# Score rows placed later between the convolution's taps, and one normalised operand made by VectorE

## The reference, cut to what matters

```python
x = x + L0(_gn(x))                      # Mamba
x = x + L1(_gn(x))                      # relu(conv3x3(batchnorm(.))) + ., then conv1x1
x = x + L2(_gn(x))                      # attention, below
x = x + L3(_gn(x))                      # bilinear shift, then 1x1

def _gn(v, G=32, eps=1e-05):            # two channels of one image form a group
    ...
    return ((g - m) / jnp.sqrt(s + eps)).reshape(v.shape)

def _L2_conv_ref(x, w1, b1, a1, w2, b2, a2, wa, ba, aa):
    e1 = _conv1x1(x, w1, b1, a1).reshape(N, -1, HW)       # prelu(w1 x + b1), 32 channels
    e2 = _conv1x1(x, w2, b2, a2).reshape(N, -1, HW)
    asm = _conv1x1(x, wa, ba, aa).reshape(N, C, HW)
    score = jax.nn.softmax(jnp.einsum('nci,ncj->nij', e1, e2), axis=2)
    return jnp.einsum('nij,ncj->nci', score, asm).reshape(N, C, H, W)
```

## Time and profile before

| what | value |
|---|---|
| median of 3 runs | 696.53 us (693.73 to 700.42) |
| span of the profiled execution | 697.9 us |
| TensorE (PE) busy | 625.1 us, 90% |
| VectorE (DVE) busy | 535.1 us, 77% |
| ScalarE (ACT) busy | 429.5 us, 62% |
| GpSimd (POOL) busy | 385.2 us, 55% |
| chain that ended last, by engine | PE 58%, DVE 19%, issue 8%, ACT 7%, POOL 4% |
| mean granted TensorE clock | 0.972 of full speed |

### The profile page before, as it was taken

One profiled execution on the slowest core, in us unless ns is written; L12 is line 12 of the kernel. 1 busy time (PEld: TensorE's weight loads), 2 busy tenths in 40 slices (PEclk: granted clock), 3 DMA queues, 4 the chain that ended last, 5 costly groups with the idle time before them and its releaser, 6 DMA issues.

```text
span 697.9 us, 8622 instructions
## 1 busy us (share of the span) xinstructions
PE 625.1 (90%) x2812; PEld 275.6 (39%) x2812; DVE 535.1 (77%) x857; ACT 429.5 (62%) x737; POOL 385.2 (55%) x243
## 2 busy tenths in 40 slices
PE   3795888888789989999989999999999999986996
PEld 1232332233353332234434444343444444335982
DVE  6996899999934465888858787887878888685547
ACT  2478689899644331235555765748476565787772
POOL 2454788887512140216939779595968979430000
PEclk9997999999999997999989999999999999998999
DMA  9000000000015482404003040300304020200006
GB/s 328 7 0 0 1 0 0 0 0 0 1 45 140 112 199 54 106 1 91 0 1 90 1 91 0 71 21 9 83 0 91 0 31 1 30 1 0 1 1 241
DMA packets 28533, 32.36 MB, mean 46 GB/s; under 512 B 16976, under 2 KB 17104, under 8 KB 28368
## 3 DMA queue, kind: packets, MB, share of 16 engines
q1 hardware_dynamic: 27056, 27.33, 15.3%
q10 hardware_dynamic: 1440, 4.55, 2.7%
HBM read 5.83 MB, written 4.19 MB: 14 GB/s over the span
## 4 chain that ended last, share of the span: by engine, by line
PE 58%; DVE 19%; issue 8%; ACT 7%; POOL 4%; DMA 1%; SPq 1%; DVEq 0%; POOLq 0%; ACTq 0%
PE PS L1723 15%; PE PS L1710 10%; PE PS L1688 9%; PE PS L1599 5%; DVE RB L476 3%; PE PS L1608 2%; PE PS L1677 2%; PE PS L1743 2%; DVE RB L552 2%; DVE PS L544 2%; DVE RB L851 2%; DVE RB L559 1%; PE PS L1850 1%; DVE SM L456 1%; DVE SM L692 1%
## 5 line engine op out<-in xcount | busy, mean ns | idle before, releaser
L692 DVE TENSOR_REDUCE SM<-PS 128x1 f32<-128x512 f32 x256 | 165.0, 683 | 65.3 <-PE PS L1688 64.7
L1154 ACT ACTIVATE RB<-PS 128x512 f32<-128x512 f32 x256 | 138.9, 594 | 88.0 <-PE PS L1710 86.9
L1391 POOL TENSOR_TENSOR RB<-RB 128x1024 f32<-128x1024 f32 x60 | 141.1, 2372 | 7.1 <-DVE RB L721 4.8
L1710 PE MATMUL PS<-R 98*128 98x512 f32 x256 | 95.5, 452 | 1.3 <-ACT RB L1154 1.3
L1688 PE MATMUL PS<-R 96*128 96x512 f32 x256 | 88.7, 418 | 6.9 <-DMA R<-R 3.2
L1723 PE MATMUL PS<-RB 128*64 128x512 f32 x320 | 85.4, 616 | 0.0
L1710 PEld LDWEIGHTS PS<-R 98*128 98x128 f32 x256 | 38.8, 189 | 83.4 <-ACT RB L1154 53.9
L1526 PE MATMUL PS<-RA,W 128*128 (+1 forms) x128 | 63.1, 636 | 8.7 <-DVE RB L552 5.3
L1688 PEld LDWEIGHTS PS<-R 96*128 96x128 f32 x256 | 48.7, 193 | 43.1 <-DVE SM L692 18.9
L1391 POOL TENSOR_TENSOR EX<-EX,RB 128x1024 f32<-128x1024 f32 x24 | 56.5, 2373 | 0.8
L1723 PE MATMUL PS<-RB,RA 128*64 128x512 f32 x192 | 52.7, 627 | 0.0
(11 more groups left out here) (186 smaller groups left out, 1111.7 us busy)
## 6 DMA issues: line engine op xcount, KB each, us to landing
R<-WS SPq DMA_DIRECT2D x72, 128.0 KB, 2.4
X<-x SPq DMA_DIRECT2D x8, 512.0 KB, 7.4
RB<-RB SPq DMA_DIRECT2D x32, 128.0 KB, 4.0
RB<-RB ACTq DMA_DIRECT2D x14, 280.5 KB, 4.1
out<-X SPq DMA_DIRECT2D x7, 512.0 KB, 2.7
R<-R SPq DMA_DIRECT2D x20, 128.0 KB, 2.4
W<-pack SPq DMA_DIRECT2D x1, 1072.0 KB, 11.6
R<-R ACTq DMA_DIRECT2D x4, 128.0 KB, 3.3
```

The costliest lines, as they stand in the source:

```text
L692: v.tensor_reduce(MX[:, par, tile, h:h + 1], bank(2 + h), AX.X, ALU.max)\
L1154: act(slot[:, h * HALF:(h + 1) * HALF], bank(4 + h), ACT.Exp).then_inc(s["p_ready"], 1)
L1391: i = g.tensor_tensor(out, out, PT[j % SLOTS][par], ALU.add)
L1710: mm(bank(4 + h), stack(b, par, 1)[0:98, j * P:(j + 1) * P], stack(b, par, 0)[0:98, h * HALF:(h + 1) * HALF]).then_inc(s["t_mm"], 1)
```

## The change

Two edits.

`FILLS` becomes `{5: (7, 4), 6: (0, 14), 7: (0, 14)}`: the first rows of pair 0 stand at slot 7 of turn 5, not at slot 3, and turns 6 and 7 take 14 rows each, not 12 and 13. The 32 rows stay 32.

`GB[0]` of pair 3 is made by VectorE, right behind `coefs_shift(GN2B, ...)` and ahead of its part of `attend(1)`. It counts in a semaphore of its own, `gb_third`, for which TensorE waits ahead of `operands(3)`. The wait for `coef_ready`, which stood ahead of `normed(3)` on GpSimd, stands ahead of `normed(4)` and its followers.

```diff
--- before.py
+++ after.py
@@ -254,7 +254,7 @@
             return bank(7 if isinstance(p, int) and (p, h) == (PAIRS - 1, 1) else 5)
 
         SLOTS1 = 9
-        FILLS = {5: (3, 7), 6: (0, 12), 7: (0, 13)}
+        FILLS = {5: (7, 4), 6: (0, 14), 7: (0, 14)}
 
         def fills_at(p, slot):
 
@@ -298,7 +298,7 @@
             dt_mm b_mm c_mm o_mm v_mm e_done dta_read u_done dt_read nd_done ln_done dt_done dtx_done
             b_read da_done scan_done c_read hc_done y_done y_last sq_done r_done normed0 blk0_done sums_done
             g1_ready ua_done ub_first ub_done shifted_even shifted_odd moved_even moved_odd conv_mm y1_done w1_mm x1_done
-            minus_done gb_ready z_mm z_read zf_done hi_done lo_done stack_in stack_low asm_mm asm_done v_part v_done
+            minus_done gb_ready gb_third z_mm z_read zf_done hi_done lo_done stack_in stack_low asm_mm asm_done v_part v_done
             s_mm s_read m_ready
             mrow_mm m_copied t_mm p_ready pv_done first_added add_done add_dve sum_mm ln_sum rec_done acc_read x2_done
             g3_pool g3_dve g3_act hat_d hat_abs hat_done am_zero am_in am_dve am_act tr_mm tr_act tr_dve s1_mm s1_copied s2_mm s2_copied
@@ -825,6 +825,8 @@
                                                 6: lambda: end7(0), 7: lambda: link(end7(1)), 10: gather,
                                                 12: lambda: coefs_var(GN2B, 3, PAIRS)})
             coefs_shift(GN2B, 3, PAIRS)
+            v.wait_ge(s["asm_mm"], 2)
+            v.tensor_scalar(GB[0], X[:, 3, :], SC[:, 3:4], SH[:, 3:4], ALU.mult, ALU.add).then_inc(s["gb_third"], 1)
             for p in range(1, PAIRS - 1):
                 attend(p, p % 3)
 
@@ -1391,9 +1393,6 @@
                         i = g.tensor_tensor(out, out, PT[j % SLOTS][par], ALU.add)
                     i.then_inc(s["add_done"], 1)
                     g.wait_ge(s["add_done"], 6 * p + j - 1)
-                    if j == 7 and p == 0:
-                        g.wait_ge(s["coef_ready"], GN2B + 1)
-                        normed(3)
 
             def clear(k):
                 g.memset(RB[:, k * L:(k + 1) * L], 0.0).then_inc(s["am_zero"], 1)
@@ -1421,6 +1420,7 @@
             g.wait_ge(s["y1_done"], 2 * PAIRS)
             for p in range(PAIRS):
                 if 0 < p < PAIRS - 3:
+                    g.wait_ge(s["coef_ready"], GN2B + 1)
                     normed(p + 3)
                 if p == PAIRS - 2:
                     g.wait_ge(s["t_mm"], 32 * (PAIRS - 2))
@@ -1653,7 +1653,10 @@
 
             def operands_free(q):
 
-                t.wait_ge(s["gb_ready"], q + 1)
+                if isinstance(q, int) and q == 3:
+                    t.wait_ge(s["gb_third"], 1)
+                else:
+                    t.wait_ge(s["gb_ready"], q if q > 3 else q + 1)
                 if isinstance(q, int) and q < 2:
                     need(t, s["v_done"], 2 * q)
                 else:
```

## The result

The changed kernel takes 692.34 us in the median of 20 runs (689.05 to 694.53), the kernel before 698.85 us in the median of 20 (692.78 to 701.18). The ratio is 0.9915, with a 95% interval of 0.9897 to 0.9932: 5.9 us less by the ratio, 6.5 between the medians, and 7.8 us above the predicted 684.5, outside of the predicted range of 681 to 690.

What follows compares the result with a forecast made beforehand. TensorE was taken to lose time only at two waits and the half clock behind them. Gains of 7.8 and 5.0 us sum to 12.8, from 697.9 to 685.1; median put at 684.5 us, range 681 to 690.

Steps and rivals of the forecast that it cites:

- What bounds the kernel: TensorE stands still for nothing in the attention, 40.14 us from pair to pair; gains lie only at seam A and seam B.
- The rows later: Turn 5: row 0 moved to slot 7, reached after its operands land, so wait and clock fall go: -7.8 us.
- Rivals 2, 3 and 4: Turns 6/7 pauses drop clock, 689.1 (0.12); clock stays down, slower (0.04); stack late, wait moves to slot 7, 692 (0.04).
- seam A: Turn 5, first row of pair 0: TensorE idles 3.17 us for a stack DMA, then half clock; 7.8 us to win.
- I take the lower end, for two reasons: Operand on VectorE put at 0.81 us, not 3.2, because recorded starts put it ahead of GpSimd's addition.
- seam B: Step 2 of attend(1): TensorE waits for GpSimd's normed(3), then half clock; costs 5.4 us, forecast gain 5.0.
- The bound from above: The operand on VectorE waits out one whole GpSimd addition: 2.4 + 0.8 = 3.2 us.
- Rival 1: Seam B: GpSimd's addition goes first, TensorE idles 2.7 us; 686.8, or 689.7 if the clock falls; chance 0.2.
- the sum: Seam A and seam B together: -7.8 - 5.0 = -12.8 us, taking the profiled execution from 697.9 to 685.1.

Runs made afterwards that it cites:

- e2: Changed kernel with the old FILLS table, so only the operand of pair 3 moves to VectorE: 698.24 us, ratio 1.0009 to before.
- e1: Kernel before with only the new FILLS table, the operand of pair 3 staying on GpSimd: 691.03 us, ratio 0.9909 to before.
- e5: Changed kernel with a product of two SBUF tiles in place of the tensor_scalar, values of pair 3 wrong: 688.66 us, one run.
- e4: Kernel before with the new FILLS table and the operand still on GpSimd, one addition earlier: 687.16 us, ratio 0.9846 to before.
- e3: Changed kernel, but GpSimd holds its last two additions of pair 0 until VectorE has made the operand: 686.86 us, ratio 0.9850 to before.
- e10: e4 with a table that starts the rows at slot 5 of turn 5: 687.00 us, ratio 0.9830 to before.
- e7: Changed kernel, but ScalarE makes the operand of pair 3, behind the exponentials of step 0 of attend(1): 687.42 us, ratio 0.9863 to before.
- e8: Changed kernel, but VectorE makes the operand one step later, behind the maxima of step 0 of attend(1): 686.58 us, ratio 0.9855 to before.
- e9: e4 with a table that starts the rows at slot 6 of turn 5: 687.10 us, ratio 0.9833 to before.

## Why the prediction was wrong, point by point

**What bounds the kernel: right.** The `operands` of pairs 4 and 5 stay 40.10 to 40.15 us apart in all twelve profiles. What was won or lost stands at the two seams.

**"The rows later": right in mechanism and place.** No idle ahead of the first row; 1.11 and 0.41 us of pauses for 1.5 and 0.4; S1 is 8.2 us shorter for 7.8. Rivals 2, 3 and 4 did not come: in the profiled execution the clock stays at its upper level, 2.4 GHz, from 250 to 300 us, and the wait did not move to slot 7.

**The size of that term was high for a median run.** 4.6 of the 7.8 us was clock, read from one execution. e2 waits at the same place, for 3.22 us, and its clock costs far less: its S1 is 47.32, 3.0 less than before's 50.27 with the same distribution of the rows. So of 4.6 us it lost 1.6. e1's ratio puts the whole of seam A at 6.3 us (4.7 to 8.0). The prediction saw that a median run may have less to win, and took 0.8 us off for it: 684.5 is 12.0 below 696.53.

**The base was off by about two us.** The prediction set the span of 697.9 beside the median of 696.53 as 1.4 above. The span leaves out 1.8 us of the device's time, so this execution is 699.7, 3.2 above that median. Over 20 runs the median of before is 698.85, and the execution is 0.9 above it. Of three runs spread over 6.7 us the median is itself no better known than by some us.

**"I take the lower end, for two reasons" is the step that failed.** The term is the operand on VectorE, put at 0.81 us; it took 2.93, the maxima behind it came late, and seam B, put at -5.0 us, came to +1.7 in the profile. The bound from above was right: the tensor_scalar waits for a whole addition, 2.93 us against the bound of 3.2. Both reasons were read from recorded starts. "The new operation is 0.03 us behind it, ahead of the addition" came true to 0.01 us, and it lost nevertheless. The other, L429 at 29.78, was an operation on two slices of `SM` and without a scalar column, beside another operation of GpSimd. It is of the kind that won in e5; the new one is of the kind that lost in after and e2. Even without e5 the text could have seen that a margin of 0.03 us between two engines' records carries no decision, and it gave the other outcome 0.2.

**Rival 1's cost came, at its upper end,** though by the records the addition was not first. It had the operation at 3.2 us and the idle at 2.7; they are 2.93 and 1.99. With the clock's fall it had 689.7, that is 6.8 us below the 696.53 from which it started; measured are 6.5 below 698.85. So of the 2.6 us between 689.7 and 692.34 the base makes 2.3. Its single terms were off in both directions: the clock's part was put at 2.9 us, as in before, and in the profile of after S2 is 7.0 us over e4's floor of 84.95, of which 2.0 is the idle and 5.0 the clock (10 us at its lower level). That profile is the slowest run of after, so the median run lost less; that its single terms add up to the right total is in part luck.

**The seam's price was about right.** Where it does close (e3, e4), S2 falls by 4.8 and 5.35 us against before's 90.30, for the 5.0 of the sum. Both seams together, S1 and S2 of e4, are 13.5 us below before's, for 12.8. By its ratio e4 is 10.7 us faster (9.3 to 12.1): that is what the change could have brought. From e1 to e4, seam B alone, it is 3.9 in medians, for the 5.0 of the sum.

## What to carry to other kernels

An operation that moves from GpSimd to VectorE can stay on the same lock, as it did here: ask what GpSimd runs at that time, take the length of that instruction as the price, and do not decide by which of two records begins first. Look at what queues behind the moved operation before where it is needed; `GB[0]` had three us to spare, the maxima behind it none, and a place one step later, or the old engine one addition earlier, cost next to nothing (S2 of 85.50 and 84.95). A loss by the clock that one execution shows is one draw: between two kernels with the same stall it was 1.6 and 4.6 us in turn 5, and 5.0 and none at step 1 of `attend(1)`, so price it with both ends. Ask too where in the spread of its kernel the profiled run lies.

## What the runs showed of the hardware

The recorded start of a VectorE operation with scalar columns does not say who goes first: 0.02 us ahead of GpSimd's addition it lost by 2.1 us in two profiles, and without the columns it won at 0.01 to 0.02, in one profile each.

Small operations wait too. L444, 128x5, took 0.99 to 1.06 us in the rows shown here, and ended as GpSimd's addition did (in e3 at 338.79, the addition before the held ones at 338.77), while L429 takes 0.16.

The clock's answer to one stall is not fixed. After 1.99 us of idle it was at 0.50 for 10 us in after and stayed at 1.00 in e2; after 3.17 and 3.22 us at the same place it fell for 10 us in before and for about 3 in e2; after 2.41 us in e1 it fell for some 3.4. After 1.11 (after) and 1.42 us (e10) it did not fall. What else decides is open.

What stays open, too, are the 2 us between the 10.7 that e4 gains by its ratio and the 12.8 of the sum: e3, e4, e7, e8, e9 and e10 lie between 686.58 and 687.42 us, and their profiles differ by more at the start of the kernel than at the two seams.
